# Half of DVE's weight quarters to POOL, the last threshold of a step taken without DVE's clip, and new order lists, in a five-engine decoder kernel

## What is computed

```python
for _ in range(3):                                   # NUM_STEPS
    scores = einsum('bhsd,hnd->bhsn', xi, K) * beta  # 8 heads, 256 memory entries
    w = entmax15(scores)
    xi = einsum('bhsn,hnd->bhsd', w, V)
# entmax15: x = (x - max(x)) / 2; find tau so that sum(clip(x - tau, 0)^2) = 1
#           return square(clip(x - tau_star, 0.0, None))
```

## Time and profile before

| | us |
|---|---|
| median of 3 runs | 892.58 (891.53 to 894.0) |
| the profiled execution, its own time | 891.69 |
| its span, first to last instruction | 889.9 |
| mean granted TensorE clock | 0.975 of full |

### The profile page before, as it was taken

One profiled execution on the slowest core, in us unless ns is written; L12 is line 12 of the kernel. 1 busy time (PEld: TensorE's weight loads), 2 busy tenths in 40 slices (PEclk: granted clock), 3 DMA queues, 4 the chain that ended last, 5 costly groups with the idle time before them and its releaser, 6 DMA issues.

```text
span 889.9 us, 18293 instructions
## 1 busy us (share of the span) xinstructions
PE 816.0 (92%) x5598; PEld 697.7 (78%) x5598; DVE 770.2 (87%) x1955; ACT 738.2 (83%) x1787; POOL 493.2 (55%) x2306
## 2 busy tenths in 40 slices
PE   7999998799999989999997999998999998998962
PEld 6878887588798878888876888787888877877751
DVE  4799998999999999989998999999899999996331
ACT  3599897989988999888899799989979899986420
POOL 4144446654565665676466656575675747765223
PEclk9999999899999989999999999999999999999986
DMA  8900120000000000000000000000000000000001
GB/s 279 212 1 1 37 72 4 12 5 7 1 1 1 2 1 1 1 3 1 26 0 1 11 13 1 1 2 1 2 22 2 1 20 1 8 1 1 2 1 33
DMA packets 24215, 17.63 MB, mean 20 GB/s; under 512 B 11760, under 2 KB 23536, under 8 KB 23856
## 3 DMA queue, kind: packets, MB, share of 16 engines
q1 hardware_dynamic: 23872, 16.13, 6.4%
q0 software_dynamic: 240, 0.27, 0.2%
HBM read 14.30 MB, written 2.10 MB: 18 GB/s over the span
## 4 chain that ended last, share of the span: by engine, by line
PE 52%; DVE 23%; ACT 15%; POOL 6%; issue 4%; DMA 0%; SPq 0%; POOLq 0%; DVEq 0%
PE banks L1257 20%; PE banks L1280 10%; DVE moments L816 9%; ACT work L726 6%; PE banks L1340 5%; PE banks L1268 5%; PE banks L1304 4%; DVE top L796 4%; PE banks L1128 3%; ACT work L717 3%; ACT work L738 2%; DVE work L836 2%; PE banks L1314 1%; ACT work L733 1%; PE banks L1332 1%
## 5 line engine op out<-in xcount | busy, mean ns | idle before, releaser
L816 DVE BATCH_NORM_STATS2 moments<-work 128x6 f32<-128x512 f32 x576 | 376.7, 687 | 8.0 <-ACT work L726 3.7
L726 ACT ACTIVATE work<-work,neg_u 128x256 f32<-128x256 f32 x768 | 334.2, 522 | 28.5 <-DVE neg_u L828 20.5
L1257 PE MATMUL banks<-weights_s,work 128*128 128x256 f32 x1536 | 352.9, 383 | 3.6 <-ACT work L717 2.4
L1257 PEld LDWEIGHTS banks<-weights_s,work 128*128 128x128 f32 x1536 | 286.8, 191 | 46.0 <-issue 7.0
L717 ACT ACTIVATE work<-banks,neg_low 128x256 f32<-128x256 f32 x384 | 155.9, 499 | 3.8 <-DVE neg_low L807 3.6
L948 POOL TENSOR_TENSOR resid_sum<-moments 128x8 f32<-128x8 f32 x144 | 30.3, 211 | 218.4 <-DVE moments L816 217.5
L796 DVE MAX8 top<-banks 128x8 f32<-128x256 f32 x384 | 140.6, 413 | 11.2 <-PE banks L1257 10.9
L1268 PE MATMUL banks<-ident,work 128*128 128x128 f32 x768 | 113.3, 283 | 21.1 <-ACT work L738 11.5
L738 ACT ACTIVATE work<-banks 128x512 f32<-128x512 f32 x192 | 113.6, 612 | 14.2 <-PE banks L1268 14.1
L1268 PEld LDWEIGHTS banks<-ident,work 128*128 128x128 f32 x768 | 90.4, 145 | 38.9 <-issue 20.4
L1280 PE MATMUL banks<-weights_s,work 128*128 128x256 f32 x512 | 115.9, 381 | 1.0 <-ACT work L738 1.0
(11 more groups left out here) (155 smaller groups left out, 1087.9 us busy)
## 6 DMA issues: line engine op xcount, KB each, us to landing
work<-in_L_xattn_Wo_dram SPq DMA_DIRECT2D x2, 1024.0 KB, 11.3
out_dram<-work SPq DMA_DIRECT2D x16, 128.0 KB, 1.8
work<-in_L_xattn_w_kc_q_dram SPq DMA_DIRECT2D x2, 768.0 KB, 5.5
rows<-in_L_xattn_Wq_dram SPq DMA_DIRECT2D x1, 1536.0 KB, 14.1
rows<-in_x_dram SPq DMA_DIRECT2D x1, 1536.0 KB, 6.9
work<-in_L_attn_Wq_dram SPq DMA_DIRECT2D x1, 1024.0 KB, 9.6
work<-in_L_attn_Wo_dram SPq DMA_DIRECT2D x1, 1024.0 KB, 14.3
work<-in_ctx_dram SPq DMA_DIRECT2D x32, 32.0 KB, 2.2
```

What stands on the lines that cost most here:

```text
L726: ins = nc.scalar.activation(q_resid[:, j, h, :], q_resid0[:, j, h, :], ACT.Relu, bias=small["neg_u"][:, j, h:h + 1])
L816: ins = nc.vector.bn_stats(moments[:, j, 2 * q:2 * q + 2, :].rearrange("p h k -> p (h k)"), r.rearrange("p h n -> p n h"))
L1257: ins = nc.tensor.matmul(ps_scores[:, h, :], lhsT, w[:, h, t, :], start=(t == 0), stop=(t == CT - 1))
```

## The change

- `DVE_WEIGHTS` goes from 2 to 1 and `POOL_WEIGHTS` = 1 is new. DVE keeps quarter 0, ACT takes quarters 1 and 2 (still two), POOL takes quarter 3 in a new stage `pool_weights`: two `tensor_scalar` (add, max) of 128 x 256 f32 from `q_resid0` to `q_resid`, with the threshold as an operand per row. In POOL's order of a tile the stage comes after `newton` of e = 2, so behind L981, L983 and L985.
- The clip of e = 2 is gone. All three engines that make weights wait for POOL's L977 itself (the semaphore `pool_step`) and read `neg_u_raw`.
- PE waits for quarter 3 on `pool_step` instead of `resid_ready`.
- The lists of all engines are new. DVE's has 1326 entries instead of 1422, POOL's 503 instead of 455; those of PE and ACT have as many as before in another order, and the last 49 entries of PE's and the last 16 of ACT's are as they were.

```diff
-DVE_WEIGHTS = 2
+DVE_WEIGHTS = 1
+POOL_WEIGHTS = 1
...
-            dve += four("moments", s, e) + once("inverse", s, e) + once("clip", s, e)
+            dve += four("moments", s, e) + once("inverse", s, e)
+            dve += once("clip", s, e) if e < EVALS - 1 else []
...
-        act += four("act_weights", s)[DVE_WEIGHTS:] + four("square_weights", s)
+        act += four("act_weights", s)[DVE_WEIGHTS:4 - POOL_WEIGHTS] + four("square_weights", s)
+        pool += four("pool_weights", s)[4 - POOL_WEIGHTS:]
...
+            def last_threshold(eng, p, j, s):
+
+                eng.wait_ge(pool_step[j], pool_count(p, s, EVALS - 1, 11))
...
-                        act.wait_ge(u_ready[j], eval_count(p, s, EVALS - 1))
+                        last_threshold(act, p, j, s)
...
-                                                       bias=small["neg_u"][:, j, h:h + 1])
+                                                       bias=small["neg_u_raw"][:, j, h:h + 1])
...
-                        dve.wait_ge(u_ready[j], eval_count(p, s, EVALS - 1))
+                        last_threshold(dve, p, j, s)
...
+                    elif stage == "pool_weights":
+
+                        last_threshold(pool, p, j, s)
+                        for h in (2 * q, 2 * q + 1):
+                            ins = nc.gpsimd.tensor_scalar(q_resid[:, j, h, :], q_resid0[:, j, h, :],
+                                                          small["neg_u_raw"][:, j, h:h + 1], 0.0, ALU.add, ALU.max)
+                        ins.then_inc(pool_step[j], 1)
...
+                            pe.wait_ge(pool_step[j], pool_count(p, s, EVALS - 1, 14 + q - (QUARTERS - POOL_WEIGHTS) + 1))
```

More of the change, by code:

```diff
@@ L186, in tile_turns @@
     return {
[L187 to L205, removed]
-               "edcdfafdffcccf9dfecfafdcefcfeeefdcafebffffbdfdffdfddeeebcbefeccefdcefffeceddcdecfefffbefefeefbdfefef"
-               "edcefbfdddcfdaffdfdeedfdfdffdeeedcdedeeedcefecfffceefeefefeffdeeeedcfefebeceffffdfdfddfcffffefffedee"
-               "deedffeecffffgefdffegf",
@@ new lines, in tile_turns @@
+        "ACT": "hhhhhhhh01h00000h020101110h00h0h22h2h2h0h0h11h110020h11112h02211h010100h21222h01000h222h121110h002h1"
+               "01h121h03h2222110h22212h033h33010h223333h0223h33h311110020121022323231331114653220000212110000337230"
+               "1003002220333311131333804444033330231344212411143330314044430234944455554204331252024024554423533344"
+               "443555333566136264410366664451556655767167753a4661616555576776715515466454746675525547172b5544455664"
+               "5562672477474456657656227542426644777676334647764747453556457367276337673535788577884656484378758585"
+               "65546884578778474646476788c65898999788679996595668688899699578758979884daa5aa5699759a5aaa88889aaaae8"
+               "889898989a7aa7a69976577989886798999688a6876b8bb9ba8698698a8aa9babb77b9aa9f88a8b88a999798bbba7aaab99b"
+               "96bbc9cccbbaa799987aab7cc97cbcbaba99cc9cc99aabaa9bbba88acaccabb7bcddb8dcdc89bbabb8ca8aca8cc8dbdbddca"
+               "acacacaddaddcccbcb9b89dbcddccd9ace9ebdebd99beb99bbbbaddadcdebecebbebbadddbadcece9eeaaccbdaeaedfffefe"
+               "cceddfcebfcafebfdeededdffffdcdcbcffcffddbfdeefdeecbbcfbfcbffecceeeffcffeddeeeddfbfeffedcddfdcfcfefee"
+               "efdddfcdcdeeeefdfcffcececeefdfefdedecfeeddfffedfdddfeffefefedefeeeefffefffffff",
@@ new lines, in tile_turns @@
+        "POOL": "hh000010100122201111122000220201110011222232033133121322hh3hh000310211102022003033121323013343414314"
+                "3433001444252553324045453324463656506635441661767705557475514556665717444667122446676544757545277355"
+                "32677466768388555884634768777588269699364997887899645a59aa884aa8887aa799957899a8687859698b8b5b98aaab"
+                "8b89a6a99b9bba6879ac97cac69c9c7bb9bacaaacbbca79bba8b87ddcdaccaddacc8dcdbcabdbb989bbce9ebebdddb8ecead"
+                "ab9deeccfecffada9dcffdcdffeefecbbcaeedfcdffbedefefcddfbffeddeeedfccefefdfeeceffcddfefbdfedefeeffgdfc"
+                "fef",
@@ L226, in tile_turns @@
+        "SP": "1205370463b28a91756c4fd98ebdacef",
     }
@@ L720, in run @@
                     elif stage == "resid":
-                        act.wait_ge(u_ready[j], eval_count(p, s, e - 1))
+                        act.wait_ge(u_ready[j], clip_count(p, s, e - 1))
                         if (p, j, s, e, q) == (0, 1, 0, 1, 0):
```

48 lines of the change are left out of this document (27 added, 21 removed).

## The result

The changed kernel takes 898.29 us (median of 7 runs, 896.72 to 899.97), the kernel before, run beside it, 894.0 us (7 runs). The ratio is 1.0052, 95% interval 1.0036 to 1.0068: slower by half a percent, where I had forecast 0.7% faster. The profiled execution has a span of 895.3 us, 5.4 us more than that of before. The rest lies outside the span: in the seven runs of the changed kernel 2.4 to 3.3 us pass outside it, in the kernel before 1.8 in every run whose span is on record. So about 1.2 us of the loss lies outside the span, and no run shows what they are.

The account below looks back on a forecast made before the run. PE was taken to bound long stretches, DVE and ACT those where PE starves. Terms: -10.4 (DVE) - 2.0 (handover) + 5.2 (POOL) + 1.2 (overlap) = -6.0 us, so 886.6 us, range 880 to 891 (8 in 10: 872 to 900).

Parts of the forecast that it names:

- What bounds it: Whole kernel: PE in long stretches, DVE and ACT where PE starves; DVE time counts 0.27 on the chain.
- Removed from DVE: Quarter 1's weights and the clip of e = 2 leave DVE: 40.3 us less work, 10.4 us less on the chain.
- the handover: Last threshold no longer passes through DVE's list; ACT's L733 idles 11.1 us for the clip: 2.0 us gained.
- The lists: New order of the engines' instruction lists: taken as nought, with 3 us to either side.
- Added to POOL: 96 tensor_scalar at 0.5 us, 48 us in all, at POOL's rate of 0.11: 5.2 us lost (ends 2.2 and 11).
- the overlap: DVE instructions met by the new wide POOL work: 4.6 us of DVE, 1.2 us lost on the chain.
- Quarter 3 as a late quarter: POOL ends quarter 3 1.75 us after the threshold, ACT 2.1: cost nought, between -0.4 and +0.6 us a step.
- DVE and POOL in each other's way: Wide POOL work delays DVE's instructions: 1.2 us on the chain; up to 48 us if every pair met DVE's.
- the port rival: POOL's pair costs DVE's pair of the same tile its whole length, 48 us: +5.3 us, 898; chance 0.12.
- the forecast case: Whole kernel: the terms sum to -6.0 us, giving 886.6 us, range 880 to 891; chance 0.42.
- POOL's list becoming the slow loop: Weight pairs in POOL's fixed list delay other tiles' sums or newton: +12 us, 904 to 905; chance 0.14.
- Its signs: In the new profile: a POOL pair with more than 12 us on the chain, or longer L726 waits for thresholds.

Follow-up runs that it names:

- the idle-work kernel: Changed kernel's lists with quarter 3 made by DVE; POOL still runs its two tensor_scalars, into a spare tile that nobody reads: 907.84 us, ratio 1.0169.
- The priced phases: Changed kernel plus rows of instructions behind the last store, POOL and DVE working at once; POOL's eight tensor_scalars took 9.06, 8.96 and 8.94 us.
- pairs in two of four slots: Changed kernel, but POOL makes both heads of quarter 3 only in slots 0 and 2, DVE in slots 1 and 3: 895.53 us, 1.0046.
- the joined and the parted instruction: Changed kernel with head 6 on DVE, head 7 on POOL, plus one spare POOL tensor_scalar: directly behind head 7 897.63 us, apart from it 902.79 us.

## Why the prediction was wrong

*What bounds it: right.* The chain did change hands with DVE's load, and relief was worth what its share of the chain said. In the new lists DVE at 759.1 instead of 735.8 us costs 6.0 us, 0.26 for each us; in the old ones 0.22, within a wide interval. I had 0.27.

*Removed from DVE, and the handover: right in kind, a little large.* I had -12.4 us for all of it. The kernel without any POOL work gives -9.6 (0.9892); the clip and its handover, tried in the old lists, give 2.5 instead of 4.0. ACT's wait, which I let end earlier, does so without POOL's pair: 8.2 us on L988 in the kernel without POOL work, against 11.1 on the clip. With the pair it is 13.7.

*The lists: right*, within the 3 us that I had given them (0.9963 against 0.9972 for the same split).

*Added to POOL: this is the step that failed*, twice. The duration: I took 0.5 us an instruction from two tensor_tensors and named 1.06 as the far end; it was 1.15, so 110 us instead of 48. I had reasoned from the number of wide inputs, and no row of that kind of instruction stood in the trace. And the rate: I multiplied by POOL's average share of the chain, 0.11, up to any size. The runs show a bend instead: up to about 55 us, spread evenly over the tiles, nothing or little, then 0.26 to 0.33 for each us. 110 us at 0.11 would have been 12.1 us; with my own terms the sum is -12.4 + 12.1 + 1.2 = +0.9, close to no change. The measured part is 0.0160 x 892.5 = 14.3 us above no POOL work. Against the forecast of -6.0 the result is 0.0052 x 892.5 = +4.6, a miss of 10.6: the duration is 6.9 of it (12.1 instead of 5.2), the rate 2.2 (14.3 instead of 12.1), the relief that came out smaller 2.8, less the 1.2 that I had counted apart for the overlap. What the added work did, in the place of a wait covered by POOL's idle time, was to hold up POOL's small steps for other tiles: DVE waits 41.0 us for them, 19.4 without it.

*Quarter 3 as a late quarter: the premise failed*, since the pair takes 2.3 us and not 1.0: with the 0.75 us before it, quarter 3 ends about 3.05 us after the threshold, and ACT's had ended after 2.1. PE waits 10.0 us for L1002, where I had said under 3. How much of the time that is by itself the runs don't separate; the idle-work kernel shows that the loss is there without it.

*DVE and POOL in each other's way: less than I took.* L847's mean is 355 ns, 350 in the kernel without POOL work, far from the 0.6 us of the port rival, and DVE's busy time is 0.4 us above that kernel's where I had 4.6. I had read the harm from L1032, a tensor_tensor, and here too the kind matters: 50.3 us of tensor_tensor cost DVE 13.4 us. The Trainium skill, SBUF — State Buffer, section Who interferes with whom, has the later one block fully until the first is done, where both want the ports that they share. The priced phases agree that DVE's tensor_scalar can be slowed by POOL (0.58 us each in one phase, 0.38 in another), and disagree on "fully", for two of DVE's went through for each one of POOL's.

*The range of the forecast case was added up wrong.* With POOL's upper end of 11 us in place of 5.2 and 3 us for the lists, 886.6 becomes 895.4, not 891; even so 898.3 lies above it, as 110 us of POOL work lie above the 101 that I had as the end.

*The rivals.* What came true is the one that I had called POOL's list becoming the slow loop, at 0.14. Its signs came too: L1002 has 6% of the chain, over 50 us where I had named 12, and ACT's idle time before L737, nearly all of it for thresholds, is 37.1 us against 28.5 before L726. The port rival's 898 is the measured time to the microsecond, but by chance, for L847 shows none of what it rests on. Of the slow loop I had written that it decides when more than 12.4/48 = 26% of the new POOL time is on the chain, or 18% at 70 us. At 110 us the break-even is 11%, today's own share, so it had to come out at or above nought. Its evidence against, the 217.5 us of waiting in front of L948, was read as free room. A part of it was: with 56 us more in single instructions POOL still waits 169.0 us there, and the time hardly moves. With 110 us it still waits 136.0 and the time rises. Idle time of an engine with fixed order isn't room for anything that comes just before its small steps are due.

*Still open:* why pairs in two of four slots cost 12.3 us more than the same totals spread evenly. What fits the kernels of the table is that the first 1.15 us of POOL's time in one step of one tile is free and the second isn't, wherever it stands: by that, half of the changed kernel's 14.3 us and 3.1 for the 11.8 us more on DVE would give 10.2 above no POOL work, and 13.7 was measured. But DVE's visits are uneven in that kernel too, and no run changes the one without the other, so this is argued and not shown. Open too are the 4.1 us between the joined and the parted instruction, the two heaps of times of the kernel without the last clip, and the 1.2 us outside the span.

## What to carry to other kernels

Price a moved instruction by a row of its own kind on that engine, and if there is none, let the upper bound go above the dearest relative, or measure it: here 0.5 against 1.15 us moved the sum from -6.0 to +0.9. An engine's share of the chain is a fair exchange rate for small reliefs (0.27 forecast, 0.22 and 0.26 measured), but it was none here for added load (POOL from nought to 0.3 where the share said 0.11, ACT 0.7 where it said 0.18). Look at who waits for the small steps of the engine that is to help, before and after: here those waits sorted the kernels, and POOL's idle share did not. And a helper that takes half of what it is offered may beat both ends: one head on POOL is 0.9% faster than before, two are 0.5% slower, none are 0.4% faster.

## What the runs showed of the hardware

- On POOL a tensor_scalar with two operations costs 0.30 us at 8 columns and 1.15 at 256, some 3.3 ns a column, and a tensor_tensor of 256 columns 0.69, a copy 0.35. Taking away one operation saves 0.25 us, taking the operand as an immediate 0.12.
- On DVE the same tensor_scalar takes 0.26 us in the pairs of the earlier trace rows; beside POOL's it took 0.58 in one phase and 0.38 in another. POOL's own eight took 9.06 us beside it and 8.94 beside bn_stats.
- POOL's tensor_tensor is the worse neighbour. With 50.3 us of it DVE's busy time is 749.2 us, 13.4 above the kernel without POOL's work, for the same instructions on DVE (the 96 L847 32.5 us instead of 29.5, the 48 small L842 13.6 instead of 9.6); with 110 us of tensor_scalar it is 736.2, or 0.4 above.
